# A decoder layer in fp32 on one core: where GpSimd's weight sums stand in the gate/up loop, and how an integer part is taken

## The chip, the cores and the metric

One core of one Trainium2 chip runs the whole program. The metric is the device time of one execution in microseconds (us), the median of several runs. A core has TensorE (matrix products, into PSUM), VectorE, ScalarE (one function per element), GpSimd and SyncE, whose queue issues all the DMAs here. Every engine works off its own list of instructions in order, and they meet at semaphores.

## What is computed

The reference is one post-norm decoder layer on x of shape (2, 512, 1024): windowed attention with 32 query and 8 key/value heads, a product with a context matrix through fake quantisation, and a ternary feed-forward network, with a layer norm behind each. Only the last part is touched. Cut to what matters:

```python
xf = x / 128.0
gate = xf @ w_gate.T                 # 2752 x 1024, every weight is -s, 0 or +s
up = xf @ w_up.T
inter = silu(gate) * up
inter_q = trunc(clip(inter * 128.0, -128.0, 127.0)).astype(int8)
down = inter_q @ w_down.T
out = trunc(clip(down * 128.0, -128.0, 127.0)).astype(int8)
x = layernorm(x + out)
```

## The kernel before

The attention, the context product and the preparation of the weights fill the first 1100 us. What follows is the feed-forward part, for ternary weights (another path for other weights exists and isn't taken). Its 2752 inner features are cut into 22 chunks of 128, gate and up together. Chunks 0, 1 and the short last one are handled ahead of the loop ("early"), chunks 2 to 20 (G_FIRST to G_LAST) by a loop over n.

A chunk multiplies a 256 x 1024 block of weights (gate and up) with 1024 tokens. By a Strassen-like scheme it takes seven half-size products G1 to G7 in place of eight; each is 8 matmuls of 128x512 (half_product, lines 1230 to 1236: the input's high and low parts, four times each), so a chunk is 56 matmuls. The order on TensorE (chunk_of, line 1273) is G1, G6, G3 of the chunk before, G2, G7, G5, G4. Three of the products take the weights as loaded (tile gq, two buffers of 8 KB), four take sums or differences of quarters of the block. GpSimd makes those four, S3, S2, S1, S4, into tile ws (weight_sums, lines 2182 to 2201): S3 feeds G7, S2 feeds G6, S1 feeds G5, S4 feeds G3. ws has one slot for each, so GpSimd waits until the chunk before has used a slot: S3 and S2 go after G7 of chunk n-1, S1 after its G5, S4 after its G3.

The results are combined on VectorE, the left 512 tokens and the right 512 tokens of a chunk being two "units". For each unit: ScalarE takes silu of the gate (unit_silu, line 1805), VectorE multiplies by up (unit_product, line 2701), ScalarE takes the absolute value (unit_size, line 1816), VectorE takes the integer part with its sign (unit_truncate, lines 2712 to 2724, four dependent steps on 128x512 fp32 in SBUF), and ScalarE stores 127 - value, held at zero from below, as uint8 (unit_store, line 1821). VectorE's list for chunk n (chunk_units, lines 2782 to 2794) is: up of the left unit of n-1 (left_up, line 2775), its product, its truncation, the sum of line 2761 for chunk n (second_sum2; it needs G6 and a copy of G1 that ScalarE makes in keep_p1, line 1852), gate of the right unit of n-1 (right_gate, line 2780), its product, its truncation, the sums of lines 2765 (third_sum2) and 2770 (right_up). ScalarE's list (lines 1862 to 1870): size of the left unit, keep_p1, store of the left unit, silu right, silu left of chunk n, size right, store right.

TensorE waits in chunk_products (lines 1250 to 1271): G6 for ws S2 and an old product, G3 for line 2770 and S4, G2 for keep_p1, G7 for line 2761 and S3, G5 for S1. SyncE (load_next, lines 882 to 886) loads the weights of chunk n when G4 of chunk n-2 is done, and in the same loop d_near, the first 8 chunks of the down weights. The other 14 (d_far, lines 921 to 925) take the place of tiles that G4 of chunk 20 reads last, and so are issued behind it. The last chunk and the joined short chunk have lists of their own (last_units, lines 1872 and 2796; lines 1386 to 1390). Then the down projection runs (down_half, line 1281): 8 tiles of 128 tokens, 2 halves, 22 matmuls each. It waits for d_far before c = 8 and c = 15.

The four steps of the truncation, and the helpers they call:

```python
then(1, dve.tensor_scalar(u_round[:, :], sizes, 128.0, ROUND, ALU.min, ALU.add))   # 2721
then(2, rounded_up(sizes, u_round[:, :], sizes))      # (r - ROUND) > size, line 2688
then(3, integer_part(sizes, u_round[:, :], sizes))    # (r - ROUND) - that, line 2691
with_sign(sizes, sizes, u_val[:, e, :])               # sign bit of u_val, line 2694
```

Of the kernel before, what the change touches and what calls it, by code (L numbers as in the profile page):

```python
# [8 lines left out]
U32 = mybir.dt.uint32  # L9
# [26 lines left out]
ROUND = 12582912.0  # L36
QMAX = 255.0
# [19 lines left out]
D_NEAR = 8  # L57
# [11 lines left out]
def build(nc, x_rows, x_cols, w_att, ctx_rows, x1_scale, x1_zp, x2_scale, x2_zp, w_gu, w_down, out):  # L69
    with ExitStack() as stack:  # L70
# [121 lines left out]
        ws = place("ws", [P, 4, SEQ], F32R, fast(16))  # L192
# [20 lines left out]
        d_near = place("d_near", [P, D_NEAR, DM], BF16, fast(24))  # L213
        d_far = place("d_far", [P, FC - D_NEAR, DM], BF16, fast(104))
        lhs = [place(f"lhs{e}", [P, FC, P], BF16, fast(132 + 6 * e)) for e in range(2)]
# [126 lines left out]
        one_path = [sem(f"one_path{k}") for k in range(37)]  # L342
# [28 lines left out]
        u_signed = next(of_fast)  # L371
        u_stored = next(of_fast)
# [163 lines left out]
        S1, Z1, S2, Z2, R1, R2, S12, NZ2S, NZ1S, KNZ2, SIZE_G, SIZE_U, SIZE_D, INV_G, INV_U, INV_D, SIZE_G128, SIZE_D128, TOP, TOP128, UNROUND = range(21)  # L536
# [48 lines left out]
        U_STEPS = 3  # L585
# [22 lines left out]

        def g_bank(n, k):

            first = 4 if n % 2 == 0 else 0
            return bank(first + {G1: 0, G2: 0, G6: 1, G7: 1, G5: 2, G3: 2, G4: 3}[k])

        def g_weight(parity, k):
# [4 lines left out]
            return ws[:, {G7: S3_SLOT, G6: S2_SLOT, G5: S1_SLOT, G3: S4_SLOT}[k], :]  # L619
# [54 lines left out]
        def _(sp):  # L674
# [225 lines left out]
            with sp.If(path == 0):  # L900
# [15 lines left out]
                with sp.Fori(2, G_LAST // 2) as r:  # L916
                    for odd in range(2):
                        load_next(r * 2 + odd, odd)
                    load_down(r - 2)
                load_next(G_LAST, 0)  # L920
                sp.wait_ge(g_done, g_at(G_LAST, G4))
                for c in range(D_NEAR, FC - 1):
                    sp.dma_start(d_far[:, c - D_NEAR, :], u_dn[c + 3]).then_inc(ud_late[(c - D_NEAR) // 7], 16)  # L923
# [35 lines left out]
        def _(pe):  # L959
# [321 lines left out]
            def down_half(t, k, half, first):  # L1281

                for c in range(FC):
                    if first and t == 0 and half == 0 and c in (D_NEAR, D_NEAR + 7):
                        late = (c - D_NEAR) // 7
                        pe.wait_ge(ud_late[late], 16 * (7 + late))
# [134 lines left out]
        def _(act):  # L1421
# [380 lines left out]
            def unit_silu(u, e, source):  # L1802

                wait(act, u_product, u - 1)
                act.activation(u_act[:, e, :], source, ACT.Silu, scale=param(SIZE_G128)).then_inc(u_silu, 1)  # L1805

            def joined_silu(u, e, source):

                wait(act, u_product, u - 1)
# [3 lines left out]
            def unit_size(u, e):  # L1813

                act.wait_ge(u_product, u + 1)
                act.activation(u_size[:, e, :], u_val[:, e, :], ACT.Abs).then_inc(u_sized, 1)  # L1816

            def unit_store(u, e, c, b):

                act.wait_ge(u_signed, u + 1)  # L1820
                act.activation(inter[:, c, b * SEQ:(b + 1) * SEQ], u_size[:, e, :], ACT.Relu,  # L1821
                               bias=param(TOP), scale=-1.0).then_inc(u_stored, 1)
# [199 lines left out]
        def _(pool):  # L2022
# [159 lines left out]
            def weight_sums(n, parity, loads):  # L2182

                g = plain(gq[parity][:, :, :])
# [813 lines left out]
```

## Time and profile before

| what | us |
|---|---|
| median of 3 runs (1541.4 to 1544.08) | 1541.88 |
| the profiled execution, its own time | 1543.53 |
| its span, first to last instruction | 1541.8 |
| TensorE busy over the span | 1455.5 (94%) |
| VectorE busy | 1085.5 (70%) |
| ScalarE busy | 734.2 (48%) |
| GpSimd busy | 753.6 (49%) |
| mean granted TensorE clock, 1.0 is full | 0.992 |

Busy times don't say what bounds a stage: matmuls overlap, so TensorE looks busy for 389 ns of each matmul although the next starts 227 ns after it. The rows below are single instructions in order of time, with a start in us from the beginning of the span and a duration. In brackets stands the time for which the engine sat idle before it, and whose instruction ended that. A tile name without a number stands for all its buffers; an instruction in a helper bears the helper's line.

### The profile page before, as it was taken

Reading aid. Unit: us, or ns where it says so; the run is one execution under the profiler, and the core shown is the slowest. Engines: PE = TensorE matmul, PEld = TensorE weight load, DVE = VectorE, ACT = ScalarE, POOL = GpSimd, SP = SyncE. Lnnn points to the kernel's source line nnn. Section 1 sums busy time; section 2 is a strip of 40 time slices with the busy share of each in tenths; the row PEclk is TensorE's granted clock in tenths of the full one; section 3 lists DMA queues with packets and bytes.
Section 4 is the critical chain, followed back from the end, with each engine's and each line's share of the span. In section 5 each row is a group of like instructions: output and inputs, shape, how many; then the busy total and the mean of one; then the engine's idle time right before and its main releaser. Section 6 shows DMA issues by size and latency. Waiting matters only on the chain. (4 is left out here: it accounts for less than half of the span.)

```text
span 1541.8 us, 23361 instructions
## 1 busy us (share of the span) xinstructions
PE 1455.5 (94%) x7332; PEld 1175.1 (76%) x7349; DVE 1085.5 (70%) x1810; ACT 734.2 (48%) x1472; POOL 753.6 (49%) x651
## 2 busy tenths in 40 slices
PE   8899999999999999999999999999789888888896
PEld 6688888888888888888888888876567666666543
DVE  7644444445566677787777777867777888888798
ACT  5433333334444566665656566735642222323374
POOL 0577777776555545555545545535844343333100
PEclk9999999999999999999999999999999999999998
DMA  6477777776744667657576767711312212121511
GB/s 218 165 278 278 277 276 276 273 274 234 237 163 167 248 226 236 244 195 278 170 266 204 252 227 249 241 74 42 123 69 73 78 61 95 61 88 62 203 43 70
DMA packets 105883, 281.11 MB, mean 182 GB/s; under 512 B 12769, under 2 KB 13153, under 8 KB 105825
## 3 DMA queue, kind: packets, MB, share of 16 engines
q1 hardware_dynamic: 105824, 280.41, 52.1%
q8 instruction: 28, 0.46, 0.1%
q14 instruction: 31, 0.25, 0.0%
HBM read 184.94 MB, written 95.42 MB: 182 GB/s over the span
## 5 line engine op out<-in xcount | busy, mean ns | idle before, releaser
L1004 PE MATMUL ps<-xo_h,wb_h 128*128 128x512 f32 x644 | 251.4, 390 | 5.6 <-ACT c L1452 2.4
L1005 PE MATMUL ps<-xo_l,wb_h 128*128 128x512 f32 x644 | 250.6, 389 | 0.0
L1006 PE MATMUL ps<-xo_h,wb_l 128*128 128x512 f32 x644 | 250.6, 389 | 0.0
L1072 PE MATMUL ps<-wo_h,o_h 128*128 128x512 f32 x512 | 206.4, 403 | 0.2 <-DMA wo_l<-wo_low 0.2
L2074 POOL TENSOR_TENSOR pm_l<-pt_l,upto 128x512 fp32r<-128x512 f32 x64 | 82.6, 1291 | 251.0 <-DVE pt_l L2365 251.0
L1073 PE MATMUL ps<-wo_l,o_h 128*128 128x512 f32 x512 | 199.8, 390 | 0.0
L1074 PE MATMUL ps<-wo_h,o_l 128*128 128x512 f32 x512 | 199.6, 390 | 0.0
L1004 PEld LDWEIGHTS ps<-xo_h,wb_h 128*128 128x128 f32 x644 | 120.9, 188 | 33.4 <-issue 6.1
L2047 POOL TENSOR_TENSOR wb_l<-wf_l,wb_h 128x512 fp32r<-128x512 f32 x66 | 87.8, 1330 | 112.5 <-DVE s_sum L2289 56.6
L1006 PEld LDWEIGHTS ps<-xo_h,wb_l 128*128 128x128 f32 x644 | 120.9, 188 | 25.3
L1005 PEld LDWEIGHTS ps<-xo_l,wb_h 128*128 128x128 f32 x644 | 120.9, 188 | 24.8
L1447 ACT ACTIVATE wb_h<-wf_l 128x512 fp32r<-128x512 f32 x69 | 43.6, 632 | 197.6 <-DVE wf_l L2294 82.2
L1496 ACT ACTIVATE prob<-prob,exp_bias 128x128 f32<-128x128 f32 x256 | 99.8, 391 | 77.4 <-DVE exp_bias L2352 77.4
L2375 DVE TENSOR_TENSOR resid<-ps,resid 128x512 f32<-128x512 f32 x128 | 88.3, 690 | 51.2 <-PE ps L1074 47.1
L2047 POOL TENSOR_TENSOR wb_l<-raw,wb_h 128x512 fp32r<-128x512 f32 x66 | 89.0, 1350 | 62.1 <-DVE wb_l L2278 48.4
L1234 PE MATMUL ps<-t_h,ws 128*128 128x512 f32 x228 | 91.3, 400 | 26.1 <-DVE c_u L2761 26.1
L1074 PEld LDWEIGHTS ps<-wo_h,o_l 128*128 128x128 f32 x512 | 96.1, 188 | 21.3
L1072 PEld LDWEIGHTS ps<-wo_h,o_h 128*128 128x128 f32 x512 | 96.5, 188 | 16.9 <-DMA wo_l<-wo_low 0.4
L1073 PEld LDWEIGHTS ps<-wo_l,o_h 128*128 128x128 f32 x512 | 96.6, 189 | 15.8
L1821 ACT ACTIVATE inter<-u_size,prm 128x512 f32 (+1 forms) x44 | 31.7, 721 | 157.1 <-DVE u_size L2694 157.1
L2063 POOL TENSOR_TENSOR q_l<-q_raw,q_h 128x512 fp32r<-128x512 f32 x64 | 83.3, 1302 | 21.4 <-ACT q_h L1474 21.4
L1234 PE MATMUL ps<-xb_h,gq 128*128 128x512 f32 x184 | 76.1, 413 | 14.7 <-ACT c_p L1852 14.7
(247 smaller groups left out, 3775.0 us busy)
## 6 DMA issues: line engine op xcount, KB each, us to landing
raw<-w_att SPq DMA_DIRECT2D x47, 512.0 KB, 5.5
f_raw<-w_gu SPq DMA_DIRECT2D x44, 512.0 KB, 5.1
u_gu<-f_unit SPq DMA_DIRECT2D x42, 512.0 KB, 4.9
gq<-u_gu SPq DMA_DIRECT2D x42, 512.0 KB, 3.7
wp_raw<-w_att SPq DMA_DIRECT2D x32, 512.0 KB, 5.8
wo_high<-wp_h SPq DMA_DIRECT2D x32, 512.0 KB, 2.8
wo_low<-wp_l SPq DMA_DIRECT2D x32, 512.0 KB, 4.2
q_rows<-c SPq DMA_DIRECT2D x64, 256.0 KB, 2.8
```

The lines of the kernel that those rows point to most:

```text
L1004: pe.matmul(prod_ps[i], wh, chunk(xo_h[i], c), start=(i in OPENS and c == 0), stop=False, skip_group_check=True)
L1005: pe.matmul(prod_ps[i], wh, chunk(xo_l[i], c), start=False, stop=False, skip_group_check=True)
L1006: last = pe.matmul(prod_ps[i], wl, chunk(xo_h[i], c), start=False, stop=(c == KH - 1), skip_group_check=True)
L1072: pe.matmul(into, oh, wo_h[half][:, h, :], start=(h == 0), stop=False)
L1073: pe.matmul(into, oh, wo_l[half][:, h, :], start=False, stop=False)
L1074: last = pe.matmul(into, ol, wo_h[half][:, h, :], start=False, stop=(h == GROUP - 1))
L1234: pe.matmul(dst, w[:, c * P:(c + 1) * P], chunk(xh, c), start=(start and c == 0), stop=False, skip_group_check=True)
L1496: last = act.activation(prob[:, par, a, :], prob[:, par, a, :], ACT.Exp, bias=exp_bias[:, par, a:a + 1], scale=SCALE, accum_out=row_sum[:, ...
L2047: pool.tensor_tensor(wb_l[i][:, :], weight_source(odd, i), plain(wb_h[i][:, :]), ALU.subtract).then_inc(w_low, 1)
L2063: pool.tensor_tensor(q_l[:, j % 2, :], q_raw[:, :], plain(q_h[:, j % 2, :]), ALU.subtract).then_inc(q_low, 1)
L2074: pool.tensor_tensor(pm_l[:, :, 0, :], pt_l[:, :, :].bitcast(F32), upto[:, :].unsqueeze(1).to_broadcast([P, TPB, P]), ALU.mult)
L2375: dve.tensor_tensor(resid[:, t, cols], source, resid[:, t, cols], ALU.add).then_inc(y_added, 1)
```

## The change

Four edits, all in the path for ternary weights.

The weight sums on GpSimd are cut into single functions and put in another order: S1 and S4 of chunk n wait for the product of the left unit of n-1; S3 of chunk n+1 waits for the end of that unit's truncation, S2 of n+1 for the product of the right unit. S3 and S4 get a second slot in ws, which grows by 4 KB per partition. For the room d_near shrinks from 8 to 6 chunks, d_far grows from 14 to 16, and the tile lhs moves up by 4 KB.

The truncation takes three steps on VectorE: the first clamps the size to at least 0.25, and subtracts 0.25 and adds 2^22 in one number, which rounds to halves; the second shifts the bits right by one and left by one, which clears the half; the third takes 2^22 off and multiplies by the sign.

ScalarE makes that sign (Sign, into the buffer that silu had used), so a later silu in that buffer waits for the end of the truncation. It also caps the value at 128, which step one no longer does, with one more Relu ahead of the store.

In VectorE's list the sum of line 2761 moves from behind the left unit's truncation to ahead of it (chunk_units only; last_units keeps its order).

```diff
--- before.py
+++ after.py
@@ -34,6 +34,7 @@
+HALVES = 4194304.0
@@ -54,7 +55,7 @@
-D_NEAR = 8
+D_NEAR = 6
@@ -189,7 +190,7 @@
-        ws = place("ws", [P, 4, SEQ], F32R, fast(16))
+        ws = place("ws", [P, 6, SEQ], F32R, fast(16))
@@ -210,9 +211,9 @@
-        d_near = place("d_near", [P, D_NEAR, DM], BF16, fast(24))
+        d_near = place("d_near", [P, D_NEAR, DM], BF16, fast(28))
-        lhs = [place(f"lhs{e}", [P, FC, P], BF16, fast(132 + 6 * e)) for e in range(2)]
+        lhs = [place(f"lhs{e}", [P, FC, P], BF16, fast(136 + 6 * e)) for e in range(2)]
...
@@ -369,6 +370,7 @@
+        u_raised = next(of_fast)
...
@@ -582,7 +584,7 @@
-        U_STEPS = 3
+        U_STEPS = 2
@@ -606,6 +608,10 @@
+        def sum_place(parity, k):
+            return {S3_SLOT: parity, S2_SLOT: 2, S1_SLOT: 3, S4_SLOT: 4 + parity}[k]
         def g_bank(n, k):
@@ -616,7 +622,7 @@
-            return ws[:, {G7: S3_SLOT, G6: S2_SLOT, G5: S1_SLOT, G3: S4_SLOT}[k], :]
+            return ws[:, sum_place(parity, {G7: S3_SLOT, G6: S2_SLOT, G5: S1_SLOT, G3: S4_SLOT}[k]), :]
         def t_part(ap, k):
@@ -913,14 +919,17 @@
-                with sp.Fori(2, G_LAST // 2) as r:
+                with sp.Fori(2, D_NEAR + 2) as r:
+                with sp.Fori(D_NEAR + 2, G_LAST // 2) as r:
+                    for odd in range(2):
+                        load_next(r * 2 + odd, odd)
-                    sp.dma_start(d_far[:, c - D_NEAR, :], u_dn[c + 3]).then_inc(ud_late[(c - D_NEAR) // 7], 16)
+                    sp.dma_start(d_far[:, c - D_NEAR, :], u_dn[c + 3]).then_inc(ud_late[(c - D_NEAR) // 8], 16)
@@ -1281,9 +1290,9 @@
             def down_half(t, k, half, first):
-                    if first and t == 0 and half == 0 and c in (D_NEAR, D_NEAR + 7):
-                        late = (c - D_NEAR) // 7
-                        pe.wait_ge(ud_late[late], 16 * (7 + late))
+                    if first and t == 0 and half == 0 and c in (D_NEAR, D_NEAR + 8):
+                        late = (c - D_NEAR) // 8
+                        pe.wait_ge(ud_late[late], 16 * (8 + late))
@@ -1801,25 +1810,29 @@
             def unit_silu(u, e, source):
-                wait(act, u_product, u - 1)
+                wait(act, u_signed, u - 1)
             def joined_silu(u, e, source):
-                wait(act, u_product, u - 1)
+                wait(act, u_signed, u - 1)
             def unit_size(u, e):
-                act.activation(u_size[:, e, :], u_val[:, e, :], ACT.Abs).then_inc(u_sized, 1)
+                act.activation(u_size[:, e, :], u_val[:, e, :], ACT.Abs)
+                act.activation(u_act[:, e, :], u_val[:, e, :], ACT.Sign).then_inc(u_sized, 1)
             def unit_store(u, e, c, b):
+                act.activation(u_size[:, e, :], u_size[:, e, :], ACT.Relu, bias=param(RAISE),
+                               scale=1.0).then_inc(u_raised, 1)
+                act.wait_ge(u_raised, u + 1)
-                               bias=param(TOP), scale=-1.0).then_inc(u_stored, 1)
+                               bias=param(FULL), scale=-1.0).then_inc(u_stored, 1)
             def early_units():
@@ -2179,27 +2192,53 @@
-            def weight_sums(n, parity, loads):
-                g = plain(gq[parity][:, :, :])
-                a11, a12, a21, a22 = g[:, 0, 0:HALF], g[:, 0, HALF:DM], g[:, 1, 0:HALF], g[:, 1, HALF:DM]
+            def sum_of(parity, k):
+                return ws[:, sum_place(parity, k), :]
+            def weight_quarter(parity, row, half):
+                return plain(gq[parity][:, row, half * HALF:(half + 1) * HALF])
+            def third_sum(n, parity, loads):
-                if isinstance(n, int) and n == G_FIRST:
-                    pool.wait_ge(x2_kept, 16 * TILES)
-                    pool.wait_ge(x2_turned, TILES)
+                if not isinstance(n, int) or n > G_FIRST + 1:
+                    pool.wait_ge(g_done, g_at(n - 2, G7))
+                pool.tensor_tensor(sum_of(parity, S3_SLOT), weight_quarter(parity, 0, 0), weight_quarter(parity, 1, 0),
+                                   ALU.subtract).then_inc(ws_made, 1)
+            def second_sum(n, parity):
+                pool.wait_ge(ws_made, s_count(n, S3_SLOT))
-                    pool.wait_ge(g_done, g_at(n - 1, G7))
-                pool.tensor_tensor(ws[:, S3_SLOT, :], a11, a21, ALU.subtract).then_inc(ws_made, 1)
-                pool.wait_ge(ws_made, s_count(n, S3_SLOT))
-                pool.tensor_tensor(ws[:, S2_SLOT, :], a22, plain(ws[:, S3_SLOT, :]), ALU.subtract).then_inc(ws_made, 1)
+                    pool.wait_ge(g_done, g_at(n - 1, G6))
+                pool.tensor_tensor(sum_of(parity, S2_SLOT), weight_quarter(parity, 1, 1), plain(sum_of(parity, S3_SLOT)),
+                                   ALU.subtract).then_inc(ws_made, 1)
+            def first_sum(n, parity):
-                pool.tensor_tensor(ws[:, S1_SLOT, :], a21, a22, ALU.add).then_inc(ws_made, 1)
+                pool.tensor_tensor(sum_of(parity, S1_SLOT), weight_quarter(parity, 1, 0), weight_quarter(parity, 1, 1),
+                                   ALU.add).then_inc(ws_made, 1)
+            def fourth_sum(n, parity):
-                if not isinstance(n, int) or n > G_FIRST:
-                    pool.wait_ge(g_done, g_at(n - 1, G3))
-                pool.tensor_tensor(ws[:, S4_SLOT, :], a12, plain(ws[:, S2_SLOT, :]), ALU.subtract).then_inc(ws_made, 1)
+                if not isinstance(n, int) or n > G_FIRST + 1:
+                    pool.wait_ge(g_done, g_at(n - 2, G3))
+                pool.tensor_tensor(sum_of(parity, S4_SLOT), weight_quarter(parity, 0, 1), plain(sum_of(parity, S2_SLOT)),
+                                   ALU.subtract).then_inc(ws_made, 1)
+            def sums_between(n, parity, loads):
+                pool.wait_ge(u_product, left(n - 1) + 1)
+                first_sum(n, parity)
+                fourth_sum(n, parity)
+                if loads is not None:
+                    pool.wait_ge(u_signed, left(n - 1) + 1)
+                    third_sum(n + 1, 1 - parity, loads)
+                    pool.wait_ge(u_product, right(n - 1) + 1)
+                    second_sum(n + 1, 1 - parity)
             def gate_up_low(slot, i, f):
@@ -2214,12 +2253,19 @@
             with pool.If(path == 0):
-                weight_sums(2, 0, 64)
-                weight_sums(3, 1, 64)
+                pool.wait_ge(x2_kept, 16 * TILES)
+                pool.wait_ge(x2_turned, TILES)
+                third_sum(2, 0, 64)
+                second_sum(2, 0)
+                first_sum(2, 0)
+                fourth_sum(2, 0)
+                third_sum(3, 1, 64)
+                second_sum(3, 1)
+                sums_between(3, 1, 96)
                 with pool.Fori(2, G_LAST // 2) as r:
-                        weight_sums(r * 2 + odd, odd, r * 32 + 32)
-                weight_sums(G_LAST, 0, G_LAST // 2 * 32 + 32)
+                        sums_between(r * 2 + odd, odd, r * 32 + (32 + 32 * odd))
+                sums_between(G_LAST, 0, None)
             with pool.Else():
@@ -2522,6 +2568,8 @@
+            dve.memset(param(RAISE), 128.0)
+            dve.memset(param(FULL), 255.0)
@@ -2718,10 +2766,11 @@
-                then(1, dve.tensor_scalar(u_round[:, :], sizes, 128.0, ROUND, ALU.min, ALU.add))
-                then(2, rounded_up(sizes, u_round[:, :], sizes))
-                then(3, integer_part(sizes, u_round[:, :], sizes))
-                with_sign(sizes, sizes, u_val[:, e, :]).then_inc(u_signed, 1)
+                halves = sizes.bitcast(U32)
+                then(1, dve.tensor_scalar(sizes, sizes, 0.25, HALVES - 0.25, ALU.max, ALU.add))
+                then(2, dve.tensor_scalar(halves, halves, 1, 1, ALU.logical_shift_right, ALU.logical_shift_left))
+                dve.scalar_tensor_tensor(out=sizes, in0=sizes, scalar=HALVES, in1=u_act[:, e, :], op0=ALU.subtract,
+                                         op1=ALU.mult).then_inc(u_signed, 1)
             def early_add(k, source):
@@ -2784,8 +2833,8 @@
+                second_sum2(n, parity)
-                second_sum2(n, parity)
```

## Rows read from the trace of the kernel before

**Rows 1.** VectorE in order of time, one round: start us, us, engine, line, operation
```profile
1324.08 0.43 DVE L2721 TENSOR_SCALAR u_round<-u_size 128x512 f32<-128x512 f32 x1 [0.70 <-ACT u_size L1816]
1324.54 1.65 DVE L2688 SCALAR_TENSOR_TENSOR u_size<-u_round,u_size 128x512 f32<-128x512 f32 x1
1326.23 0.69 DVE L2691 SCALAR_TENSOR_TENSOR u_size<-u_round,u_size 128x512 f32<-128x512 f32 x1
1326.95 0.69 DVE L2694 SCALAR_TENSOR_TENSOR u_size<-u_val,u_size 128x512 uint32<-128x512 uint32 x1
...
1328.16 0.68 DVE L2780 TENSOR_TENSOR c_u<-ps,c_u 128x512 f32<-128x512 f32 x1
1329.71 0.75 DVE L2701 SCALAR_TENSOR_TENSOR u_val<-c_low,prm,u_act 128x512 f32<-128x512 f32 x1 [0.87 <-ACT u_act L1805]
1331.16 0.98 DVE L2721 TENSOR_SCALAR u_round<-u_size 128x512 f32<-128x512 f32 x1 [0.70 <-ACT u_size L1816]
1332.17 1.66 DVE L2688 SCALAR_TENSOR_TENSOR u_size<-u_round,u_size 128x512 f32<-128x512 f32 x1
1333.87 1.67 DVE L2691 SCALAR_TENSOR_TENSOR u_size<-u_round,u_size 128x512 f32<-128x512 f32 x1
1335.57 0.69 DVE L2694 SCALAR_TENSOR_TENSOR u_size<-u_val,u_size 128x512 uint32<-128x512 uint32 x1
...
1336.97 0.69 DVE L2770 TENSOR_TENSOR c_low<-ps,c_u 128x512 f32<-128x512 f32 x1
1337.57 0.68 DVE L2775 TENSOR_TENSOR c_u<-ps,c_u 128x512 f32<-128x512 f32 x1
1338.40 0.75 DVE L2701 SCALAR_TENSOR_TENSOR u_val<-c_u,prm,u_act 128x512 f32<-128x512 f32 x1
1339.85 0.43 DVE L2721 TENSOR_SCALAR u_round<-u_size 128x512 f32<-128x512 f32 x1 [0.70 <-ACT u_size L1816]
```

**Rows 2.** Line 2775: count, shortest/median/longest ns, first and last start
```profile
L2775 DVE TENSOR_TENSOR c_u<-ps,c_u x18: 678/680/691, 1165.6 to 1431.9; 128x512 f32<-128x512 f32 x18
L2775 DVE TENSOR_TENSOR c_p<-ps,c_u x1: 691/691/691, 1441.8 to 1441.8; 128x512 f32<-128x512 f32 x1
```

**Rows 3.** TensorE in order of time, last round and joined product
```profile
1434.60 0.79 PE L1234 MATMUL ps<-xb_h,gq 128*128 128x512 f32 x1 [2.57 <-ACT c_p L1852]
...
1437.92 0.39 PE L1234 MATMUL ps<-t_h,ws 128*128 128x512 f32 x1
...
1448.58 0.39 PE L1235 MATMUL ps<-x_l,jw 128*128 128x512 f32 x1
```

**Rows 4.** Stretches of the slow matmuls: busy (x) by engine, PEclk, DMA share, GB/s
```profile
1434.60:1436.00 1.40, 1.40 (x3) 1.16 (x4) 1.34 (x2) 0.00 (x0) 0.00 (x0) 0.50 0.00 0
```

**Rows 5.** GpSimd in order of time, same round
```profile
1330.56 1.30 POOL L2192 TENSOR_TENSOR ws<-gq 128x512 fp32r<-128x512 f32 x1 [4.92 <-PE ps L1235]
...
1333.25 1.74 POOL L2197 TENSOR_TENSOR ws<-gq 128x512 fp32r<-128x512 f32 x1
```

**Rows 6.** Line 2375, attention, beside GpSimd work: count, shortest/median/longest ns
```profile
L2375 DVE TENSOR_TENSOR resid<-ps,resid x128: 677/692/693, 504.1 to 1066.7; 128x512 f32<-128x512 f32 x128
```

**Rows 7.** ScalarE in order of time, same round
```profile
1327.76 0.72 ACT L1821 ACTIVATE inter<-u_size,prm 128x512 f32 x1 [3.23 <-DVE u_size L2694]
1328.95 0.72 ACT L1805 ACTIVATE u_act<-c_u,prm 128x512 f32<-128x512 f32 x1 [0.47 <-DVE c_u L2780]
...
1339.18 0.63 ACT L1816 ACTIVATE u_size<-u_val 128x512 f32<-128x512 f32 x1 [2.09 <-DVE u_val L2701]
1339.72 0.58 ACT L1852 ACTIVATE c_p<-ps 128x512 f32<-128x512 f32 x1
```

**Rows 8.** Chain that ended last, in order of time, from 1440 us
```profile
1449.41 7.26 DMA d_far<-u_dn
```

**Rows 9.** ScalarE in order of time, first signs of the down projection
```profile
1465.18 0.59 ACT L1912 ACTIVATE y_sign<-ps 128x512 f32<-128x512 f32 x1
...
1470.45 1.28 ACT L1658 ACT_TABLE_LOAD   x1
```

More of the change, by code:

```diff
@@ L341, in build @@
         stored = sem("stored")
-        one_path = [sem(f"one_path{k}") for k in range(37)]
+        one_path = [sem(f"one_path{k}") for k in range(38)]
         of_fast = iter(one_path)
@@ L534, in build @@
         TILE_ADDED = [OUT_BLOCKS - 13, OUT_BLOCKS - 12] + [OUT_BLOCKS - 14 + 2 * t for t in range(2, TILES)]
-        S1, Z1, S2, Z2, R1, R2, S12, NZ2S, NZ1S, KNZ2, SIZE_G, SIZE_U, SIZE_D, INV_G, INV_U, INV_D, SIZE_G128, SIZE_D128, TOP, TOP128, UNROUND = range(21)
+        S1, Z1, S2, Z2, R1, R2, S12, NZ2S, NZ1S, KNZ2, SIZE_G, SIZE_U, SIZE_D, INV_G, INV_U, INV_D, SIZE_G128, SIZE_D128, TOP, TOP128, UNROUND, RAISE, FULL = range(23)
         u_gu = nc.dram_tensor("u_gu", (FC + 10, 2, P, DM), F32).ap()
```

## The prediction

> **What bounds the kernel now.** The changed code runs once per chunk of the gate/up loop, so I first looked in the view of line 2775, VectorE's first step for a chunk, for where the loop stands: it starts at 1165.6 us for chunk 2 and at 1431.9 for chunk 19 [rows 2], 17 rounds in 266.3 us, 15.66 us each. The second question is whether TensorE needs that long. In order of time, from 1437.92 to 1448.58 us it ran 48 matmuls without a gap [rows 3], 47 intervals of 0.2268 us; 56 of them are 12.70 us. TensorE has 3 us per round to spare.
>
> So I read one round of VectorE [rows 1]. From the first step of a truncation at 1324.08 to the same at 1339.85 is 15.77 us, with hardly a gap but two: for ScalarE's absolute value (0.70) and for its silu (0.87). This ring through VectorE and ScalarE is the bound. Within it the reader should see one operation with two durations: line 2688 on SBUF operands takes 1.65 or 1.66, line 2691 0.69 or 1.67, and line 2721 0.43 or 0.98. The long ones fall on GpSimd's sums. Line 2197 on GpSimd ran from 1333.25 to 1334.99 [rows 5]; line 2691, issued at 1333.87, ended at 1335.54, 0.55 us after it. GpSimd's took 1.74 there against 1.30 for line 2192: it first waited until line 2688 ended at 1333.83. Each shuts the other out. What reads PSUM is exempt: line 2375 never took more than 0.693 us in 128 instances, beside much GpSimd work [rows 6].
>
> The Trainium skill ("SBUF — State Buffer", on the engine ports) says that GpSimd and a VectorE instruction with two SBUF inputs, or in a two-port mode, hold one port pair as an exclusive lock for a whole instruction. The trace agrees: 1.67 us is a wait and then 0.55.
>
> In the round shown the lock costs VectorE 0.96 + 0.55 + 0.97 + 0.98 = 3.5 us (each duration over its short form).
>
> **The new round, step by step.** Start to start [rows 1, 7]:
> - line 2775 to the left product: 0.83;
> - product to the copy of line 1852: 1.32, and Sign ahead of the copy adds 0.54, the distance from the absolute value to what follows: 1.86;
> - copy 0.58 and 0.04 to hand over: 0.62, then line 2761, now ahead of the truncation. It also needs G6, but the copy is later;
> - line 2761 to step one: 0.60, as one sum from PSUM follows another (2770 to 2775); steps one and two at 0.43 + 0.03 each: 0.92;
> - step three to ScalarE's first Relu 0.81 (line 2694 to line 1821), that Relu 0.72 + 0.04, the store 0.63, then silu: 2.20. By way of line 2780 it would be 0.61 + 0.79 = 1.40: the added Relu puts the store on the path;
> - silu to the right product 0.76; product to step one 1.45 + 0.54 for Sign: 1.99; two steps 0.92; step three to line 2770 1.40 as now from line 2694; to line 2775 0.60.
>
> Sum: 12.70 us. The price of a step two I take from line 2721, the same kind of instruction (0.43); no row shows a shift. Its bounds are 0.43 and 0.69, the uint32 form of line 2694.
>
> What is left of the lock: S1 and S4 start when the left product ends and take 2 x 1.30, until 3.48 us behind its start. Step one stands at 1.86 + 0.62 + 0.60 = 3.08 and would end at 3.51; blocked, it ends 0.28 after 3.48 (1332.14 against the 1331.86 at which line 2192 ends). That costs 0.25. S3 starts behind step three, where line 2780 reads PSUM and VectorE then waits for silu: nothing. S2 starts with ScalarE's two functions and ends 2.14 behind the right product's start, step one would start at 1.99: nothing to 0.2. A round is then **12.95 us**, and TensorE's own 12.70 lies just under it.
>
> Work that the new waits could hold up: GpSimd's list is in order, so S2 for the next chunk ends 2.14 behind the right product, 10.2 us behind line 2775, and its reader G6 stands one TensorE round and eight matmuls behind, at 14.5. S3 needs the next weights; they are issued as now, behind G4. SyncE's list loses two small loads and gets no new wait. The silu's later condition is met, because the store ahead of it on ScalarE waits for the same truncation. The two memsets and the larger ws cost nothing here.
>
> - **Rounds:** 17 x 12.95 = 220.2 against 266.3: **-46.1**.
> - **Start:** the first copy (chunk 2) comes behind an Abs and a store, so it is 0.54 + 0.76 later, against some 0.4 that shorter truncations give back on VectorE, an estimate between nothing and one step (0.69): **+0.9**.
> - **Last round:** line 2775 to G2 is 2.67 now (1431.93 to 1434.60), then 0.83 + 1.86 + 0.62 = 3.31: +0.6. TensorE was idle for 2.57 us before G2 and the next eight matmuls took 3.32 us in place of 1.92 [rows 3]: the granted clock was 0.50 [rows 4], the lower of its two levels, 1.2 GHz. TensorE will be nearly caught up with, so this goes: -1.4. Together **-0.8**.
> - **Down weights:** the chain of waits ends the loop with the landing of d_far at 1456.67, its last issue at 1449.41 [rows 8]. G4 of chunk 20 released the first at 1441.7 [rows 2]: 14 tiles in 15 us. Two more cost from 2 x 0.48 for the issues to 2 x 1.07 for the landing, say 1.5; the wait comes one tile earlier (+0.2). TensorE then idles some 3 us, and as with the 2.57 above I count 1.4 for the lower clock. **+3.1**. What ScalarE and VectorE save behind G4 hides under this transfer.
>
> Sum -46.1 + 0.9 - 0.8 + 3.1 = **-42.9**. The profiled execution (1543.53, span 1541.8) would become 1500.6 (span 1498.9). It lies 1.65 above the median, 1541.88, which gives **1499.0 us**.
>
> **The rivals.**
> - *The shift runs at one element a cycle* (0.69): 0.26 more in each of two units, a round of 13.47, +8.8: **1507.8**. For it: no row has a shift in it, and the only integer form there takes 0.69. Against: that one has two tensors. By the Trainium skill ("Vector Engine (DVE) Microarchitecture Reference", 5.1) the two-port mode asks for SBUF on both sides and not for a type; by that, 0.43 holds. 20%.
> - *TensorE becomes the bound*, because my gaps are a little long and the round is 12.70, with no lower clock at the end: 17 x 0.25 + 1.4 less, **1493.4**. 12%.
> - *The ring doesn't close as drawn:* two or three hand-overs of 0.3 us that I don't see, 13.6 a round: +11, **1510**. 14%.
> - *Sign isn't in silu's table* and each change between them loads one. A round has two changes, 2 x 1.28 by the row of a load [rows 9], all in the ring: 15.5 a round, **1542.4**, no change. Against it: the first Sign, at 1465.18, works with the table that the loop's silus had loaded; the next load, at 1470.45, belongs to line 1658's root [rows 9]. 1%. The Trainium skill ("ScalarE: Activation LUTs", on table sets) names relu, copy, identity and abs as in every set and not sign, and puts a switch at 2.7 us with its drain: by that, 18.3 a round, and slower.
> - *Slower: the lock moves and doesn't go.* The four sums now start at VectorE's own steps. If a sum, once issued, always fell on a truncation, 4 x 1.30 = 5.2 us would join the 12.70: 17.9 a round, +38, near **1583**. It decides from 2.96 us of blocking per round on (15.66 - 12.70). For it: each sum is released by the step just ahead of locked ones. Against: by the distances above ScalarE's two functions (1.2 us) and the PSUM sums lie between, and only 0.25 is left. 2%.
>
> **How the numbers follow.** The forecast has 51%. The range takes in the faster rival, the shift and most of the open ring: 1493 to 1511. A measurement of this kernel tells 0.2% (3 us) from no change. Slower: the lock, 2%. Within 0.2%: the table, 1%. The rest is faster, 97%.
>
> **What would show it.** In the changed profile: line 2775's starts 12.9 to 13.0 us apart; no truncation step over 0.7 but the left unit's first, at about 0.7; the shift at 0.43; Sign 0.54 behind Abs with no table load; silu right behind a store and not behind line 2780; TensorE's waits for line 2761 nearly gone; a stall on d_far of about 3 us in the first down tile. Rounds above 13.3, or shifts at 0.69, make it wrong; so does a step that still takes 1.67 in every round.

## The result and the profile after

The changed kernel takes **1499.39 us** (median of 4 runs, 1497.8 to 1500.38) against 1541.64 for the kernel before on the same chip (4 runs, 1541.23 to 1544.08): a ratio of 0.972, 95% interval 0.971 to 0.974. The forecast was 1499.0 us, the range 1493 to 1511. The profiled execution took 1499.07 us, span 1497.3. VectorE's busy time fell from 1085.5 to 991.3 us, ScalarE's rose from 734.2 to 787.4, and TensorE is busy for 97% of the span instead of 94%.

First the step that counts the rounds, line 2824, which was line 2775 [rows 2]: count, shortest, median and longest ns, first and last start.

```profile
L2824 DVE TENSOR_TENSOR c_u<-ps,c_u x18: 679/680/692, 1161.8 to 1384.1; 128x512 f32<-128x512 f32 x18
L2824 DVE TENSOR_TENSOR c_p<-ps,c_u x1: 692/692/692, 1394.7 to 1394.7; 128x512 f32<-128x512 f32 x1
```

17 rounds take 222.3 us, 13.08 each, where they took 266.3 and 15.66. Four stretches make up the span: until this line first starts, the 17 rounds, the last round to the row with c_p, and the rest.

| stretch, us | before | after | measured | forecast |
|---|---|---|---|---|
| to the first start | 1165.6 | 1161.8 | -3.8 | +0.9 |
| 17 rounds | 266.3 | 222.3 | -44.0 | -46.1 |
| last round | 9.9 | 10.6 | +0.7 | -0.8 |
| from c_p to the end | 100.0 | 102.6 | +2.6 | +3.1 |
| span | 1541.8 | 1497.3 | -44.5 | -42.9 |

The total lies close to the forecast, but two of the four terms have the wrong sign. The start came 4.7 us below its term and pays for the rounds (2.1 above) and the last round (1.5 above); the span ends 1.6 us below the forecast. The median lies 0.4 above it, because the profiled execution before was 1.65 us above its median and the one after 0.3 below. That the total is so close is luck. Here is one round of VectorE in order of time (start, duration, in brackets the idle time before it and who ended it), to be held against [rows 1]:

```profile
1305.83 0.68 DVE L2824 TENSOR_TENSOR c_u<-ps,c_u 128x512 f32<-128x512 f32 x1
1306.65 0.75 DVE L2749 SCALAR_TENSOR_TENSOR u_val<-c_u,prm,u_act 128x512 f32<-128x512 f32 x1
1309.27 0.69 DVE L2810 TENSOR_TENSOR c_u<-ps,c_p 128x512 f32<-128x512 f32 x1 [1.87 <-ACT c_p L1865]
1309.88 0.51 DVE L2770 TENSOR_SCALAR u_size<-u_size 128x512 f32<-128x512 f32 x1
1310.42 0.43 DVE L2771 TENSOR_SCALAR u_size<-u_size 128x512 uint32<-128x512 uint32 x1
1310.88 0.69 DVE L2772 SCALAR_TENSOR_TENSOR u_size<-u_size,u_act 128x512 f32<-128x512 f32 x1
1311.49 0.69 DVE L2829 TENSOR_TENSOR c_u<-ps,c_u 128x512 f32<-128x512 f32 x1
1313.82 0.75 DVE L2749 SCALAR_TENSOR_TENSOR u_val<-c_low,prm,u_act 128x512 f32<-128x512 f32 x1 [1.64 <-ACT u_act L1814]
1315.79 0.62 DVE L2770 TENSOR_SCALAR u_size<-u_size 128x512 f32<-128x512 f32 x1 [1.22 <-ACT u_act L1826]
1316.45 0.43 DVE L2771 TENSOR_SCALAR u_size<-u_size 128x512 uint32<-128x512 uint32 x1
1316.91 0.69 DVE L2772 SCALAR_TENSOR_TENSOR u_size<-u_size,u_act 128x512 f32<-128x512 f32 x1
...
1318.91 0.68 DVE L2824 TENSOR_TENSOR c_u<-ps,c_u 128x512 f32<-128x512 f32 x1
```

Line 2770 is step one of the truncation, 2771 the two shifts, 2772 step three, 2749 the product, 2810 the moved sum (it was 2761). No truncation step takes longer than 0.69 here, where four were lengthened before. Step one has 0.51 and 0.62; free of GpSimd it has 0.42, as below. The shift has 0.43. GpSimd in the same round:

```profile
1307.57 1.30 POOL L2221 TENSOR_TENSOR ws<-gq 128x512 fp32r<-128x512 f32 x1 [4.52 <-DVE u_val L2749]
1308.82 1.29 POOL L2229 TENSOR_TENSOR ws<-gq,ws 128x512 fp32r<-128x512 f32 x1
...
1314.84 1.29 POOL L2214 TENSOR_TENSOR ws<-gq,ws 128x512 fp32r<-128x512 f32 x1 [1.73 <-DVE u_val L2749]
```

Each sum has its undisturbed 1.29 or 1.30. The two pairs that still touch are S4 (line 2229, until 1310.11) with step one at 1309.88, and S2 (line 2214, until 1316.13) with step one at 1315.79. In both, step one ends 0.28 after the sum, the distance that [rows 1, 5] showed. ScalarE between the two units:

```profile
1307.43 0.63 ACT L1825 ACTIVATE u_size<-u_val 128x512 f32<-128x512 f32 x1 [1.33 <-DVE u_val L2749]
1307.97 0.62 ACT L1826 ACTIVATE u_act<-u_val 128x512 f32<-128x512 f32 x1
1308.49 0.58 ACT L1865 ACTIVATE c_p<-ps 128x512 f32<-128x512 f32 x1
1311.61 0.73 ACT L1831 ACTIVATE u_size<-u_size,prm 128x512 f32<-128x512 f32 x1 [2.54 <-DVE u_size L2772]
1312.45 0.72 ACT L1834 ACTIVATE inter<-u_size,prm 128x512 f32 x1
1313.08 0.71 ACT L1814 ACTIVATE u_act<-c_u,prm 128x512 f32<-128x512 f32 x1
```

Sign (line 1826) starts 0.54 behind Abs, with no load of a table, and silu (line 1814) follows directly behind the store (line 1834), as forecast. The waits from 1190 to 1380 us (engine, line, for whom: total us, times, longest) name the ring:

```profile
DVE u_val L2749 <- ACT u_act L1814: 24.7, 15, 1.7
...
DVE c_u L2810 <- ACT c_p L1865: 20.6, 11, 1.9
...
DVE c_u L2810 <- PE ps L1244: 7.3, 4, 1.9
PEld ps L1243 <- ACT c_p L1865: 5.7, 12, 0.5
```

TensorE's one wait that this view lists is for the copy of line 1865, up to 0.5 us a round; none is for the moved sum. The view puts 4 waits of line 2810 down to TensorE, but of its products the line needs only G6, which had ended about 2 us before (at 1307.22 in the round shown), and it starts 0.67 to 0.78 us behind the start of the copy in all 15 rounds: it is the copy there too. At the loop's end stand these rows of TensorE and two windows (busy us and count of PE, PEld, DVE, ACT, POOL, then the granted clock, DMA share, GB/s):

```profile
1387.32 0.50 PE L1243 MATMUL ps<-xb_h,gq 128*128 128x512 f32 x1 [1.78 <-ACT c_p L1865]
...
1410.58 2.42 PE L1296 MATMUL ps<-d_far,lhs 128*128 128x512 bf16 x8 [2.74 <-DMA d_far<-u_dn]
```

```profile
1388.00:1390.00 2.00, 2.00 (x7) 1.50 (x5) 1.95 (x3) 0.58 (x1) 0.38 (x1) 0.50 0.00 0
```

```profile
1412.00:1414.00 2.00, 2.00 (x6) 0.70 (x5) 0.75 (x1) 1.10 (x3) 0.00 (x0) 0.50 1.05 416
```

In the last round TensorE still idled for 1.78 us and then had the lower level of its clock, 1.2 GHz (0.50), where I had counted that away. On the late down tiles, ahead of the second eight matmuls on d_far (c = 14), it idled for 2.74 us and had the lower level again. In the kernel before it idled for 0.88 us at c = 15 and kept the full clock (1.00 from 1454 to 1464 us).

### The profile page after: what moved, and what is told of

Same layout as the page of the kernel before. It is cut to its first block and busy times, and to the rows that moved or that the text cites. A ratio compares the mean times of both kernels' runs of the same rounds, so it can differ in the third digit from the quotient of the medians.

```text
span 1497.3 us, 23449 instructions
## 1 busy us (share of the span) xinstructions
PE 1445.6 (97%) x7349; PEld 1177.5 (79%) x7349; DVE 991.3 (66%) x1768; ACT 787.4 (53%) x1560; POOL 741.2 (50%) x651
## 5 line engine op out<-in xcount | busy, mean ns | idle before, releaser
L1244 PE MATMUL ps<-t_l,ws 128*128 128x512 f32 x228 | 89.0, 390 | 0.0
```

Of the source, the lines that this page charges most:

```text
L1244: last = pe.matmul(dst, w[:, c * P:(c + 1) * P], chunk(xl, c), start=False, stop=(c == KH - 1), skip_group_check=True)
```

## The experiments

Eleven runs followed, all against the kernel before on the same chip: e1 to e4 on one chip together (kernel before 1542.62), then e5 to e8 (1542.34), then e9 to e11 (1540.31). My theory was the forecast's: two independent savings in one ring through VectorE and ScalarE, the shorter truncation and the lock. The rivals: one of the two edits does it all; the moved sum is what brings the gain; or TensorE is already the bound, so nothing is left to win.

**e1, the truncation alone**: the sums on GpSimd back in the old order with their old waits (S3, S2, S1, S4), the rest as changed.

```diff
-                pool.wait_ge(u_product, left(n - 1) + 1)
-                first_sum(n, parity)
-                fourth_sum(n, parity)
...
+                        weight_sums(r * 2 + odd, odd, r * 32 + 32)
```

> The changed kernel with GpSimd's four weight sums back in the old order and behind the old waits (G7, G5, G3 of the chunk before); truncation, Sign, cap, the moved line 2761 and the 6 + 16 down tiles stay. My theory (the port lock, and where it falls): the sums fall on the truncation steps again and steps of 1.0 to 1.7 us come back; a round of 14.1 to 14.5 us against 13.08 in the changed kernel, 1517 to 1523 us. Rival (the shorter truncation is the whole gain, the order of the sums is beside the point): a round of 13.1, 1499 to 1502 us.

Measured: 1522.06 us (1519.61 to 1522.63), ratio 0.986, interval 0.984 to 0.988. Line 2791 (2824 in the change) starts 14.38 us apart. Both lie in the expected ranges. VectorE in order of time, and GpSimd:

```profile
1301.00 1.24 DVE L2716 SCALAR_TENSOR_TENSOR u_val<-c_low,prm,u_act 128x512 f32<-128x512 f32 x1 [1.65 <-ACT u_act L1814]
1303.46 1.47 DVE L2737 TENSOR_SCALAR u_size<-u_size 128x512 f32<-128x512 f32 x1 [1.22 <-ACT u_act L1826]
...
1311.47 0.42 DVE L2737 TENSOR_SCALAR u_size<-u_size 128x512 f32<-128x512 f32 x1
```

```profile
1301.77 1.62 POOL L2207 TENSOR_TENSOR ws<-gq,ws 128x512 fp32r<-128x512 f32 x1
1303.36 1.29 POOL L2210 TENSOR_TENSOR ws<-gq 128x512 fp32r<-128x512 f32 x1
```

The right unit's product takes 1.24 instead of 0.75 and its step one 1.47 instead of 0.42: 0.49 + 1.05 = 1.54 us of lock in a round. The changed kernel has 0.09 + 0.20. The difference, 1.25, is the difference of the rounds, 14.38 - 13.08 = 1.30, to within 0.05. It is not this round alone: from 1200 to 1360 us products and truncation steps take, over their short forms (0.75, 0.69, 0.43), 3.4 us a round in the kernel before, 1.6 in e1, 1.3 in e2 and 0.3 in the changed kernel.

**e2, the order of the sums alone**: the old truncation in four steps, no Sign and no second Relu, with the new order, the second slots and the moved sum.

```diff
-                then(1, dve.tensor_scalar(sizes, sizes, 0.25, HALVES - 0.25, ALU.max, ALU.add))
...
+                then(1, dve.tensor_scalar(u_round[:, :], sizes, 128.0, ROUND, ALU.min, ALU.add))
+                then(2, rounded_up(sizes, u_round[:, :], sizes))
+                then(3, integer_part(sizes, u_round[:, :], sizes))
+                with_sign(sizes, sizes, u_val[:, e, :]).then_inc(u_signed, 1)
```

> The changed kernel with the four-step truncation, the single Abs and the single Relu of before; the new order of the weight sums, the moved line 2761 and the 6 + 16 down tiles stay. My theory: no truncation step meets more than one sum, but S1 and S4 (2.6 us) begin at the left product and hold the left unit's first step for 0.8 us and the right unit's for 0.5; ring of 13.8 to 14.1 us a round, 1511 to 1517 us. Rival (the lock alone made the gain of 3 us a round): TensorE's 12.7 a round, 1493 us.

Measured: 1524.48 us (1522.49 to 1526.01), ratio 0.988, interval 0.986 to 0.990; rounds of 14.28 us. This is 7 us above the expected range. Its VectorE rows:

```profile
1323.59 0.75 DVE L2745 SCALAR_TENSOR_TENSOR u_val<-c_u,prm,u_act 128x512 f32<-128x512 f32 x1
1325.69 0.69 DVE L2805 TENSOR_TENSOR c_u<-ps,c_p 128x512 f32<-128x512 f32 x1 [1.35 <-ACT c_p L1861]
1326.30 1.03 DVE L2765 TENSOR_SCALAR u_round<-u_size 128x512 f32<-128x512 f32 x1
...
1332.44 1.13 DVE L2765 TENSOR_SCALAR u_round<-u_size 128x512 f32<-128x512 f32 x1 [0.70 <-ACT u_size L1825]
```

Without Sign ahead of it, step one comes 0.5 us sooner after the product, and so meets the sum that the product released: 1.03 and 1.13 instead of 0.43, so 1.3 us of lock a round. That is what was expected, 0.8 and 0.5, so the lock is not what was missed. The profile is 26.2 us longer than that of the changed kernel: 20.4 in the rounds, which are 0.18 over the expected 14.1 each, 3.8 from the later start (1165.6 instead of 1161.8) and 1.9 in the last round, two terms that the expectation had left out. In the changed kernel Sign stands ahead of step one and fills the time in which GpSimd has the lock. It costs the ring nothing: from 1200 to 1360 us step one ends 3.73 us behind the start of the left product in e2 and 3.74 in the changed kernel, behind the right one 2.58 and 2.59 (medians). The sum sets that moment, with Sign or without. The two savings in a round are 1.28 (e1) and 1.38 (e2), together 2.66 against the 2.58 of the whole change: in the rounds they add up. The times don't (20.6 + 18.1 = 38.7 against 43.2 for the repeat e5), and the profiles, where 6.8 us are missing, say where it goes. Behind the c_p row e1 and e2 each take 102.7 us, 2.7 more than before, with the wait on d_far and the lower clock; e5 takes 0.4 more. That is 5.0 us. The last round is 0.7 and 2.6 longer than the 9.9 before, in e5 0.6: another 2.7. The rounds and their starts bring 0.9 back. In e2's last round TensorE idled for 2.12 us before 1415.23, and the granted clock was 0.55 from 1416 to 1418. So each edit alone gives about half, and no rival of the form "one does it all" is left.

**e3 (and e9), the store later**: in ScalarE's list the left unit's cap and store move behind the right unit's silu, the next left silu and the right Abs and Sign.

```diff
-                unit_store(left(n - 1), 1, n - 1, 0)
                 right_silu(n - 1, 1 - parity, right(n - 1), 0)
                 left_silu(n, parity)
                 unit_size(right(n - 1), 0)
+                unit_store(left(n - 1), 1, n - 1, 0)
```

> The changed kernel with one edit in ScalarE's list: the left unit's cap and store stand behind the right unit's Abs and Sign and no longer between the end of the left truncation and the right silu. My theory (the ring of VectorE and ScalarE decides, 13.08 a round, and TensorE's 12.70 lies just under it): silu comes 1.4 us behind step three in place of 2.2, the ring falls to 12.2 to 12.3, TensorE becomes the bound, 12.70 to 12.75 a round: 5.5 to 6.5 us less than the changed kernel, near 1493 us. Rival (TensorE, or a slip elsewhere, already decides): no difference, 1499 us.

Measured: 1489.24 us (1487.12 to 1490.49), ratio 0.966, interval 0.964 to 0.967. Rounds of 12.69 us: 215.8 from the first start to the last, 6.5 less than in the changed kernel. The span is 11.9 us lower (1485.4): beside the rounds, 2.3 from an earlier start of them (1159.5), which the repeat e9 doesn't show (1162.7), 0.7 in the last round (9.9) and 2.4 behind it (100.2), where the clock stayed up (1.00 from 1398 to 1404 us). Who ends VectorE's waits has changed, here in the repeat:

```profile
1306.06 0.69 DVE L2810 TENSOR_TENSOR c_u<-ps,c_p 128x512 f32<-128x512 f32 x1 [2.05 <-PE ps L1244]
1306.67 0.41 DVE L2770 TENSOR_SCALAR u_size<-u_size 128x512 f32<-128x512 f32 x1
...
1308.19 0.68 DVE L2829 TENSOR_TENSOR c_u<-ps,c_u 128x512 f32<-128x512 f32 x1
1309.75 0.75 DVE L2749 SCALAR_TENSOR_TENSOR u_val<-c_low,prm,u_act 128x512 f32<-128x512 f32 x1 [0.87 <-ACT u_act L1814]
```

The gap before the right product was 1.64 and is 0.87: silu no longer waits for the cap and the store, and follows line 2829 instead. Now it is TensorE that ends the wait ahead of line 2810. The round equals the 12.70 us that the matmuls need by [rows 3]: this is the bound that the prediction held for a rival.

**e4, the late down tiles issued earlier**: SyncE issues the 16 tiles of d_far in groups behind G6, G7 and G4 of the last chunk, instead of all behind G4.

```diff
-                sp.wait_ge(g_done, g_at(G_LAST, G4))
-                for c in range(D_NEAR, FC - 1):
-                    sp.dma_start(d_far[:, c - D_NEAR, :], u_dn[c + 3]).then_inc(ud_late[(c - D_NEAR) // 8], 16)
...
+                for k, first, past in ((G6, 0, 4), (None, 12, 16), (G7, 4, 8), (G4, 8, 12)):
+                    if k is not None:
+                        sp.wait_ge(g_done, g_at(G_LAST, k))
+                    for c in range(D_NEAR + first, D_NEAR + past):
+                        load_far(c)
```

> The changed kernel with the 16 late down tiles issued in four groups, each as soon as the product that last reads its place is done (8 behind G6 of chunk 20, 4 behind G7, 4 behind G4) and not all behind G4. My theory: the stall of 2.74 us in the first down tile and the stretch at the lower clock behind it go: 4 to 4.5 us less than the changed kernel, near 1495 us. Rival (ScalarE's and VectorE's last units end at the same time, so the stall hides them): less than 1.5 us gained.

Measured: 1495.5 us (1493.91 to 1496.12), ratio 0.969, interval 0.968 to 0.971. The rounds stay as they are (222.4), the wait on d_far is gone, and from the c_p row to the end it is 97.9 us instead of 102.6.

**e5, the changed kernel again**, without an edit.

> The changed kernel once more, as the standard for the runs beside it on this chip. All theories: 1497 to 1501 us, a round of 13.05 to 13.1.

Measured: 1499.11 us (1497.53 to 1501.18), ratio 0.973, interval 0.971 to 0.975; 17 rounds again in 222.3. Its profile has no lower clock on the down tiles. TensorE's row there:

```profile
1410.97 1.90 PE L1296 MATMUL ps<-d_far,lhs 128*128 128x512 bf16 x8 [2.38 <-DMA d_far<-u_dn]
```

From c_p to the end it is 100.4 us here. So of the +2.6 us in the table 1.7 belong to a clock that does not always fall (from these eight matmuls to the next on d_far it is 4.72 us in the changed kernel and 3.03 here), and 0.4 to a longer wait.

**e6, the moved sum back** behind the left unit's truncation:

```diff
-                second_sum2(n, parity)
                 unit_truncate(left(n - 1), 1)
+                second_sum2(n, parity)
```

> The changed kernel with line 2761 (second_sum2) back behind the left unit's truncation. By my distances the move only chooses what covers S1 and S4: without it, step one comes 1.97 us behind the left product and is then held by the lock for 1.4, which is what copy, hand-over and line 2761 took: a round of 13.1 to 13.3, 1499 to 1503 us, with a left step one of 1.8 us. Rival (the move is what takes the sums off the truncation, and was needed): steps of 1.4 to 1.7 us in more than one place, a round over 13.6, 1508 us or more.

Measured: 1493.49 us (1492.94 to 1494.67), ratio 0.969, interval 0.967 to 0.971: 5.6 us **faster** than e5, the changed kernel beside it, where I had expected 0 to 4 slower. Rounds of 12.79.

```profile
1303.51 0.75 DVE L2749 SCALAR_TENSOR_TENSOR u_val<-c_u,prm,u_act 128x512 f32<-128x512 f32 x1
1305.48 0.53 DVE L2770 TENSOR_SCALAR u_size<-u_size 128x512 f32<-128x512 f32 x1 [1.22 <-ACT u_act L1826]
1306.04 1.40 DVE L2771 TENSOR_SCALAR u_size<-u_size 128x512 uint32<-128x512 uint32 x1
1307.48 0.69 DVE L2772 SCALAR_TENSOR_TENSOR u_size<-u_size,u_act 128x512 f32<-128x512 f32 x1
```

```profile
1305.69 1.47 POOL L2229 TENSOR_TENSOR ws<-gq,ws 128x512 fp32r<-128x512 f32 x1
```

From the left product to step three it is 3.97 us here and 1310.88 - 1306.65 = 4.23 in the changed kernel. The moved sum does keep the truncation off S4: put back, the shift is blocked and takes 1.40 (+0.97). But it delays step one: 3.23 behind the product (1306.65 to 1309.88) instead of the 1.97 at which Sign releases it, 1.26 more, of which steps one and two give back 1.00 (1.00 from step one to step three instead of 2.00). What is left, 0.26 us, is nearly the whole 0.29 by which the rounds differ.

**e7, no cap**: the second Relu is left out, so this kernel does not limit values to 128.

```diff
-                act.activation(u_size[:, e, :], u_size[:, e, :], ACT.Relu, bias=param(RAISE),
-                               scale=1.0).then_inc(u_raised, 1)
-                act.wait_ge(u_raised, u + 1)
```

> Leaves out the cap at 128: the added Relu is gone and the store is as before the change. My theory (this Relu lies in the ring): silu 0.8 us earlier in each left unit, the ring at 12.3, TensorE the bound at 12.70 to 12.75 a round: 5.5 to 6.5 us less than the changed kernel, near 1493 us, the same as with the later store. Rival (ScalarE's added work is off the path): no difference.

Measured: 1491.51 us (1491.41 to 1493.83), ratio 0.968, interval 0.966 to 0.970; rounds of 12.69, with line 2807 waiting for TensorE as in e3. The cap costs 0.84 us in the ring, of which 0.39 can be seen before TensorE becomes the bound. To put its work later (e3) is worth as much in the rounds as to leave it out.

**e8 to e11, both in one kernel**: e8 is e3 with e4; e9 repeats e3, e10 repeats e8, and e11 adds e6's edit to them, the last three each timed five times.

> The changed kernel with the later left store and the early down tiles together. My theory: the two gains lie in different stages and add: 9.5 to 11 us less than the changed kernel, 1488 to 1490 us. Rival (a faster loop brings the end of the loop closer to the transfers, and one eats the other): 1492 to 1494 us.

> The store-later kernel once more, beside the two below. Theory A (the ring of VectorE and ScalarE set the round, and with the store moved TensorE sets it): rounds of 12.69 us as before, the line behind the four adds starting 18 times with 215.8 us from first to last; median 1488 to 1491. The first measurement read 1489.24, with a start of the loop 2.5 us earlier than in other kernels; rival: that start was chance, and the median lies at 1491 to 1492.

> Store later and the late down tiles issued earlier. If the wait for the down tiles (2.2 to 2.7 us) is still the last thing ahead of the down projection's end, this is 2 to 4 us below the store-later kernel of the same call; rival: VectorE's and ScalarE's steps on the down results bound the end once the tiles are there, and under 1.5 us is left.

> Store later, late down tiles earlier, and the moved add (first of the right four) back behind the left truncation. Theory A: TensorE sets the round at 12.69 with or without the moved add, so the rounds stay at 215.8 us and the time is that of the kernel with both within 1 us. Rival B: the add moved back is late for the end of TensorE's round, or the lock now falls in the truncation's second step on the path, and the rounds are 12.8 or more: 2 us or more slower.

| kernel | median us (range) | ratio, interval | rounds | first start |
|---|---|---|---|---|
| e8 | 1488.19 (1486.45 to 1491.11) | 0.966, 0.963 to 0.968 | 215.8 | 1162.0 |
| e9 | 1490.47 (1489.43 to 1492.39) | 0.967, 0.966 to 0.969 | 215.8 | 1162.7 |
| e10 | 1486.88 (1486.15 to 1488.28) | 0.965, 0.964 to 0.966 | 215.8 | 1160.9 |
| e11 | 1488.21 (1485.41 to 1489.09) | 0.966, 0.964 to 0.967 | 215.7 | 1160.1 |

e8 lay 1 us below e3's time, which is from another chip. On one chip e10 is 3.6 us below e9; their times don't overlap, though the intervals of the ratios still do. Of the 4.2 us between their profiled spans, 1.8 lie ahead of the loop, where neither edit acts, and 2.4 behind it. The chain of waits behind c_p says what changed hands. First e9 from 1388 us to the end, then e10 from 1386:

```profile
by line: PE ps L1296 73.1%; SPq L932 7.3%; DMA d_far<-u_dn 7.1%; issue 1.1%; DVE rows L2987 0.8%; DVE rows L2892 0.7%; DVE y_int L2736 0.7%; DVE ln L2599 0.7%; DVE y_int L2890 0.7%; DVE y_int L2739 0.7%; ACT y_size L1924 0.7%; SPq L933 0.6%
```

```profile
by line: issue 11.5%; DVE y_int L2744 10.9%; DVE ln L2607 10.8%; DVE y_int L2747 10.7%; DVE rows L2900 7.5%; DVE y_int L2898 6.9%; DVE y_round L2895 5.6%; ACT lhs L1924 3.4%; ACT u_size L1833 2.6%; ACT u_act L1834 2.2%; DVE u_size L2780 2.1
```

In e9 the chain goes through TensorE and its wait for d_far; with the tiles there in time it goes through VectorE's steps on the down results. Counted from the c_p row, TensorE ends 2.8 us sooner in e10 and the span 2.4, so the rival (under 1.5) falls. e11 settles e6's edit: with TensorE the bound, the place of the moved sum no longer matters for the rounds (215.7). Its median is 1.3 us above e10's, where within 1 was expected, but the times overlap. The best kernel here is e10 with 1486.9 us; by the ratios, 0.965 against the 0.972 of the changed kernel, that is some 11 us below it (the medians are from different chips).

## Why the prediction was right, and where it was not

- **"17 x 12.95 = 220.2".** Measured 222.3. The steps, forecast and then measured: line 2824 to the product 0.83, 0.82; to the copy 1.86, 1.84; copy to the moved sum 0.62, **0.78**; to step one 0.60, 0.61; steps one and two 0.92 plus 0.25 of lock, 0.54 + 0.46; step three to silu 2.20, 2.20; silu to the product 0.76, 0.74; product to step one 1.99, 1.97; two steps 0.92, **0.66 + 0.46**; to line 2824 2.00, 2.00. So 0.16 too little for the hand-over of the copy, and 0.20 for S2, which I had bounded by "nothing to 0.2" and taken as nothing (it ends 2.31 behind the right product and not 2.14); 0.17 too much on the left unit, because the late copy let S4 nearly finish. One error paid for another, as both act on the same gap: that the sum came within 0.13 us of a round is in part luck. The ring itself, its steps and what bounds it, was right.
- **The truncation's price.** The shift takes 428 ns in the mean of the 29 between 1190 and 1380 us, so the 20% rival at 0.69 falls. The Trainium skill ("Vector Engine (DVE) Microarchitecture Reference", 5.1), which doesn't ask for a float type, is borne out by this row.
- **Sign's table.** One load stands ahead of the loop's silus, at 1128.04, and none between silu and Sign. The Trainium skill ("ScalarE: Activation LUTs") doesn't list sign among the functions that every set holds; for silu's set this case shows that it is there.
- **The lock.** 3.5 us a round became 0.3. e1 and e2 show it from two sides: 1.5 with the old order, 1.3 with the new order and the old truncation. The slower rival needed 2.96; the sums' places were read rightly. What the forecast did not see is that Sign, which it put into the ring with 2 x 0.54, costs nothing there (e2).
- **"Start +0.9".** Measured -3.8, and -3.0 in the repeat. The eleven profiles with the new truncation (the change, e1, e3 to e11) start the rounds between 1159.5 and 1163.2, the kernel before and e2 both at 1165.6. The step that failed is "some 0.4 that shorter truncations give back on VectorE". The -3.8 in four parts, from the rows of both kernels:
  - The first early product starts at 1130.16 instead of 1131.31: -1.15. Of the change only the two memsets stand ahead of it, and between the eleven profiles it varies from 1127.7 to 1131.4.
  - From there to the last early product it is 18.86 us instead of 21.36: **-2.50**, where the forecast has -0.4. I counted one of the early truncations, but several stand on VectorE's path. e1, with the old order of the sums, has 18.85: it is the truncation.
  - From the last early product to the first copy (1149.02 to 1152.21, before 1152.67 to 1154.59): +1.27, against the 1.30 that I had for Sign and the cap.
  - From the copy to line 2824: 9.62 instead of 11.01, -1.39. TensorE starts at the lower clock there (granted clock 0.50 to 0.60), after 4.25 us idle (5.50 before), and its matmuls come 0.43 us apart or more for 2.7 us (1152.85 to 1155.57) instead of 5.7 (1155.22 to 1160.94). In e1, idle for 4.27 us, it lasts 6.1; why it ends sooner in the changed kernel was not found.
- **"TensorE will be nearly caught up with, so this goes".** It did not. TensorE still idled for 1.78 us before G2 of the last chunk and had the lower clock after it. In the rounds it loses 0.25 us to the same copy (1308.64 to 1309.12, where 0.227 is the pace). The kernel shows what I passed over: in the last chunk the order is G1, G6, G2, G7, G4, G5 and only then G3 of the chunk before (line 1396), so that TensorE comes to the wait 8 x 0.227 = 1.8 us sooner, while the ring brings the copy no sooner. 0.25 + 1.81 = 2.06 is near the 1.94 that were lost (1385.15 to 1387.32). No run tries this alone. The step that failed is to conclude from the rounds, where TensorE is nearly caught up with, on a last chunk with another order. Where TensorE is the bound (e3, e7, e9, e10) the last round is 9.9 us.
- **"Down weights +3.1".** Measured +2.6, the wait 2.74 against "some 3". The wait is 1.9 longer than before (0.88) and the lower clock costs 1.7, but TensorE also comes to this wait 0.9 us sooner behind the c_p row (13.1 instead of 14.0). e4 takes 4.7 us from this stretch, about the whole wait and the lower clock, 2.74 + 1.7; that is more than the edit had added, because the wait of 0.9 us that the kernel before already has goes too.
- **What the forecast missed altogether** is that two parts of the change cost what they need not. It priced the cap and the moved sum correctly as links of the ring, but never asked for each link whether another order of the same list would take it out. e3 and e6 do this with one line each.

## What to carry to other kernels

Price a change by its ring, link by link, from rows of the same kind: here that came within 0.13 us of a 13.08 us round, with some luck. Then ask of each link of the new ring whether its place in an engine's list puts it there, because an added instruction in an in-order list delays all that stand behind it (the store ahead of silu: 6.5 us in all). Where two engines exclude each other, what counts is when each starts: a step in between, here Sign, can use the time of the lock and so be free, while a step put there only to dodge the lock, as the moved sum, can cost as much as it saves (1.26 us of delay for 1.00 in e6). And ask of the last round whether its list is that of the others.

## What the runs showed of the hardware that I had not expected

- A shift with one SBUF source is shut out by GpSimd just as the float steps are: 1.40 us in e6 instead of 0.43, ending 0.28 after GpSimd's sum at 1307.16. The Trainium skill ("SBUF — State Buffer") lets the one that starts first keep the port pair for the whole instruction; the 1.40 agrees.
- The lower clock after a wait did not follow from the length of the wait. Before the second eight matmuls on d_far TensorE idled for 2.23 us in e6 and the eight took 2.59 (granted clock 0.50 from 1406 to 1408 us); in the repeats e5 and e9 it idled for 2.38 and 2.64 and they took 1.90 (in e5 1.00 from 1410 to 1416 us).
- The loop's start varies by 3.7 us between the eleven profiles above, most of them alike up to there (the first early product varies as much), more than the 0.2% that a comparison is to resolve, while 17 rounds agree to 0.1 us. Rounds are the better measure of an edit in a loop.
